# Half-precision products that nobody reads, placed in TensorE's waits: the last feed-forward part of each stack, and the norm with the latents

## What is computed

```python
x = x + 0.5 * ffn_ref(layernorm(x), ...)   # a stack of 6 layers
x = x + attn_ref(layernorm(x), ...)        # latent attention, 16 heads
x = x + 0.5 * ffn_ref(layernorm(x), ...)   # the same stack again

# one layer of the stack: 16 heads of 64, keys in windows of 32
x = attn_layer(shift_tokens(x), Wqkv, qs, ksc, Wo) + x
x = ffn_layer(shift_tokens(x), g, bln, W1, b1, W2, b2) + x

def ffn_layer(x, g, bln, W1, b1, W2, b2):
    mu = x.mean(-1, keepdims=True)
    var = ((x - mu) ** 2).mean(-1, keepdims=True)
    xn = (x - mu) / jnp.sqrt(var + 1e-05) * g + bln
    hg = xn @ W1 + b1                       # 128 -> 2 * 341
    a, gate = jnp.split(hg, 2, -1)
    return a * jax.nn.gelu(gate, approximate=False) @ W2 + b2

# latent attention begins with
kv_c = x @ W_kv                             # 128 -> 32
kv_c = kv_c * rsqrt(mean(kv_c * kv_c) + 1e-6) * g_kv
q_c = x @ W_q                               # 128 -> 64
```

## Time and profile before

| | |
|---|---|
| median of 3 runs | 5265.4 us (5253.43 to 5268.99) |
| the profiled execution, its own time | 5250.07 us |
| its span, first to last instruction | 5247.9 us |
| mean granted TensorE clock | 0.951 of full speed |
| TensorE busy | 4961.6 us (95%) |
| DVE, ACT, POOL busy | 73%, 68%, 69% |
| first tail, mean product to barrier | about 2001.5 to 2035.7 us of the span |
| norm with the latents | about 2038.4 to 2102.2 us |
| second tail | about 5204.5 to 5237.8 us |

### The profile page before, as it was taken

The page is one execution under the profiler, slowest core; times in us unless marked ns, Lnnn a source line. Parts: engine busy times, 40 slices in busy tenths (PEclk is TensorE's granted clock), DMA queues, the critical chain, the costliest instruction groups (busy, mean ns, idle before and its releaser), DMA issues. The chain is left out here.

```text
span 5247.9 us, 143424 instructions
## 1 busy us (share of the span) xinstructions
PE 4961.6 (95%) x46348; PEld 3103.1 (59%) x46348; DVE 3839.2 (73%) x8399; ACT 3594.2 (68%) x10738; POOL 3597.6 (69%) x4498
## 2 busy tenths in 40 slices
PE   7999999999999997899999997999999999999998
PEld 4666666666666663344444443666666666666665
DVE  5888878888788882455555555888878888788885
ACT  4888888888888882133333332888878878788785
POOL 6988888888888882211111123988888888888884
PEclk8999999999999996598988898999999999999998
DMA  2122122221212211000000001122121221212211
GB/s 74 47 58 52 45 60 50 56 54 47 58 49 60 50 47 20 5 3 3 3 3 3 3 3 48 48 51 59 45 60 48 53 56 44 60 48 56 53 45 34
DMA packets 296849, 217.73 MB, mean 41 GB/s; under 512 B 82028, under 2 KB 293608, under 8 KB 295144
## 3 DMA queue, kind: packets, MB, share of 16 engines
q1 hardware_dynamic: 296072, 208.01, 15.8%
HBM read 40.83 MB, written 1.05 MB: 8 GB/s over the span
## 5 line engine op out<-in xcount | busy, mean ns | idle before, releaser
L541 POOL TENSOR_TENSOR inv<-ssm,neg_half 128x8 f32<-128x8 f32 x768 | 1364.3, 1776 | 119.8 <-DVE ssm L860 55.3
L555 POOL TENSOR_TENSOR rot<-t 128x256 f32<-128x256 f32 x1536 | 1124.6, 752 | 335.8 <-DVE t L849 267.2
L732 ACT ACTIVATE prob<-ps,nmx,inv 128x96 f32<-128x96 f32 x3072 | 1288.1, 434 | 55.7 <-DVE nmx L846 44.0
L628 PE MATMUL ps<-w_qkv,xs 128*128 128x512 f32 x1536 | 874.3, 652 | 59.1 <-issue 28.8
L1361 ACT ACTIVATE ptl<-ps_l 128x1024 f32<-128x1024 f32 (+1 forms) x288 | 281.2, 977 | 707.9 <-PE ps_l L1222 560.3
L835 DVE TENSOR_REDUCE mx<-ps 128x4 f32<-128x384 f32 x768 | 424.5, 553 | 385.6 <-PE ps L655 382.9
L732 ACT ACTIVATION_READ_ACCUMULATOR prob<-ps,nmx,inv 128x1 f32 x3072 | 632.1, 206 | 0.0
L725 ACT COPY vt<-ps 128x256 f32<-128x256 f32 x768 | 286.4, 373 | 470.3 <-PE ps L666 458.7
L819 DVE TENSOR_TENSOR t<-ps,tab_s 128x256 f32<-128x256 f32 x1536 | 573.1, 412 | 36.2 <-issue 28.4
L827 DVE TENSOR_TENSOR prob<-prob,rec 128x384 f32<-128x384 f32 x768 | 562.6, 732 | 26.4
L716 ACT ACTIVATE sq<-ps 128x512 f32<-128x512 f32 x768 | 472.9, 616 | 109.1 <-PE ps L628 107.4
(11 more groups left out here) (192 smaller groups left out, 8291.2 us busy)
## 6 DMA issues: line engine op xcount, KB each, us to landing
vs<-vt SPq DMA_DIRECT2D x768, 96.0 KB, 2.2
vs<-vt SPq DMA_DIRECT2D x768, 64.0 KB, 2.0
vs<-vt SPq DMA_DIRECT2D x768, 32.0 KB, 1.8
xs<-x_a SPq DMA_DIRECT2D x384, 32.0 KB, 1.9
w_qkv<-in_L_ffn_Wqkv SPq DMA_DIRECT2D x48, 256.0 KB, 3.8
w_qkv<-in_L_ffn_Wqkv SPq DMA_DIRECT2D x48, 128.0 KB, 3.1
w_o<-in_L_ffn_Wo SPq DMA_DIRECT2D x12, 512.0 KB, 4.1
w<-in_L_ffn_W SPq DMA_DIRECT2D x12, 341.0 KB
```

The source lines that it names most:

```text
L541: nc.gpsimd.tensor_tensor(inv[:, n % 4], ssm[:, n % 2], neg_half[:, 0:2 * HU], ALU.pow).then_inc(z["inv_ready"], 1)
L555: nc.gpsimd.tensor_tensor(rot[:, n % 4, half[w]], t1[:, n % 2, half[w]], t2[:, n % 2, half[w]], ALU.add).then_inc(z["rotated_" + w], 1)
L628: pe.matmul(ps[:, j % 2, :], xs[:, j // UT % 2, :], w_qkv[:, 0:2, u * 256:(u + 1) * 256], start=True, stop=True).then_inc(z["qk_ready"], 1)
L732: e = nc.scalar.activation(prob[:, n % 2, h, :], scores[:, h % 2, h // 2, :], ACT.Exp, scale=inv[:, n % 4, h:h + 1], bias=nmx[:, n % 2, h: ...
```

## The change

Two local functions `spare` issue products of the half-precision identity with itself, repeated four times: 128 rows, 512 columns out, no semaphore, result never read. In the stacks they write bank 0, which only the queries' and keys' product uses, and they are issued only in the slots `j >= UNITS + LAG_Y`, that is in the tail. The three added waits are for the last readers of banks 0 and 1. In the norm with the latents they write bank 7, which is first used by the rotation.

```diff
@@ window_stack, block.tensor
             pe.wait_ge(z["consts_ready"], 8 + 2 * (k + 1))
+
+
+            def spare(count):
+                for n in range(count):
+                    pe.matmul(ps[:, 0, :], ident_h[:, :], ident_h[:, :].unsqueeze(1).to_broadcast([P, 4, P]), start=True, stop=True)
+
+            SPARE = {"mean": 4, "var": 6, "spread": 5, "gate": 2, "up": 2, "down": 8}
 
             def feed_forward(L, p, g):
...
                 if p is not None:
                     feed_forward(L, p, g)
+                    if j >= UNITS + LAG_Y:
+                        if p == PHASE["mean"]:
+                            pe.wait_ge(z["squared"], (L + L0 + 1) * UNITS)
+                            pe.wait_ge(z["t1_ready"], (L + L0 + 1) * UNITS)
+                            pe.wait_ge(z["t2_ready"], 2 * (L + L0 + 1) * UNITS)
+                        for name, count in SPARE.items():
+                            if p == PHASE[name] or (name in ("gate", "up") and p in PHASE[name]):
+                                spare(count)
                 if live(LAG_P):
@@ latent_attention, block.tensor
+            def spare(count):
+                for n in range(count):
+                    pe.matmul(ps[:, 7, :], ident_h[:, :], ident_h[:, :].unsqueeze(1).to_broadcast([P, 4, P]), start=True, stop=True)
+
+
             for n in range(G + 2):
                 if n < G:
                     norm_mean(nc, z, pe, nb, mean_w, q0 + n, n)
+                if n == 0:
+                    spare(4)
                 if 1 <= n <= G:
                     norm_var(nc, z, pe, nb, mean_w, q0 + n - 1, n - 1)
+                if n == 1:
+                    spare(6)
                 if n >= 2:
                     latents(n - 2)
                 if 1 <= n <= G:
                     norm_spread(nc, z, pe, nb, ones_w, q0 + n - 1, n - 1)
                 if n >= 2:
                     latent_squares(n - 2)
+                    spare(6)
                     latent_spread(n - 2)
+                    if n > G:
+                        spare(4)
```

## The result

The changed kernel takes 5224.67 us (median of 7 runs, 5217.76 to 5239.88), the kernel before beside it 5262.21 us (7 runs, 5245.57 to 5268.99). The ratio is 0.9938 with a 95% interval of 0.9918 to 0.9958: faster by 0.6%, some 33 us by the ratio and 37.5 by the two medians. The profiled execution took 5234.97 us (span 5232.8), 15.1 us less than that of before; it is one of the slower of the seven, and that of before one of the faster.

A forecast was written before the change was run, and what follows sets the result against it. TensorE bounds the kernel, 95% busy, with its clock halved in places. Tails 12.4, norm 8.5 and decoding 4.5 sum to 25.4 us off the profiled 5250.07; against the median of 5265.4 that gives 5240 us, range 5223 to 5262.

The forecast's parts named there:

- The tails: Both stacks' tails: full clock gives back 17.4 us, less 2.0 for spares and 3.0 for half-clock stretches, 12.4 us.
- The eight: Spares behind each tail's down product: they delay the barrier and the mix by about 1.0 us, 2.0 for both stacks.
- one short half-clock stretch per tail: In each tail the clock still falls once for a short stretch, costing 1.5 us each, 3 us for both.
- the weakest spot: First up product in the tail: its two spares end some 2 us before the gelu lets the second up go.
- The norm: Norm with the latents, from the first latents on: faster products at full clock save 8.5 us.
- The 60%: Norm with the latents: share taken of the remaining 14.1 us, because one wait of about 1.5 us has no spares.
- The decoding: Decoding behind the norm: full clock lasts about five us of the 22.84 us at half clock, saving 4.5 us.
- every fall follows a stretch in which TensorE mostly waited: Reading of the earlier trace's clock falls, used to argue that spares filling about 60% of each tail wait hold the clock.
- an edit ahead of it may shift that by some us either way: Attention: places where the clock rises and falls hang on small shifts; some us either way, nothing booked.
- The clock falls again and again: Rival, 15%: clock falls at gelu, mix and an unfilled norm wait, returning late; 12 us less gain, 5253 us.
- The full clock throughout, decoding included: Rival, 15%: full clock holds through tails, norm and decoding until the rotation's waits; 41 us less, 5224.5 us.
- The spares stand in the way: Rival, 10%: half-precision spares fail to hold the clock and outlast waits in tails and norm; 16 us more, 5281 us.

The follow-up runs named there:

- e1_tails: The change with spares in the two tails alone, none in the norm with the latents: 5239.8 us, ratio 0.9946 against the kernel before.
- e4_no_eight: The change without the eight spares behind the down product of each tail: 5222.73 us, ratio 0.9905 against the kernel before.
- c1_tiny: The change with every spare in its place but one column wide in place of 512: ratio 0.9976 against the kernel before.
- p1_ahead: The kernel before plus 35 one-column products in the first tail alone, ahead of the second stack's loop: ratio 0.9962 against the kernel before.
- c2_after: The change itself run again, unaltered: ratio 0.9916 against the kernel before, 43 us faster.
- e2_norm: The change with spares in the norm with the latents alone, none in the tails: 5238.95 us, ratio 0.9937 against the kernel before.
- e3_rows32: The change with every spare from 32 rows in place of 128, same number, place and length: 5261.7 us, ratio 0.9978 against the kernel before.

## Why the prediction was right, and where it was not

The direction, the chance given to it and the range held. The forecast of 5240 us lies 15 us above the measured time. Part of that is 3.6 us more in the booked stages; the larger part is a gain that no term named.

**The tails (12.4 us booked).** Measured 7.2 and 6.2 us in the profiles, 13.4 together, and 13.4 again with the tails alone (e1_tails). The eight were booked at 2.0 for both; e4_no_eight gives 1.8, by the drain that was named; the mix follows the down product's end by 2.0 us, as forecast. The one short half-clock stretch per tail was there too. In the profile of the change it lies ahead of the first spares, at the last output product and the mean; in its repetition, and in 9 of the 14 tails with these spares, it follows the gelu's wait, the weakest spot that was named. Its price in the tail is the same at either place: 0.95 on the mean (2.07 against 1.12), or 0.9 on the third up (2.00 against 1.09). The longer L645 (3.05 and 3.78 against 2.05) lies ahead of the tail, and in the first stack the kernel before had 3.51 there. Booked were 1.5 a tail, the price of L638: this term was too large by about half a microsecond a tail, which accounts for 13.4 in place of 12.4.

**The norm (8.5 booked, bounds 5 to 14).** Measured 10.7, 8.6 in the repetition and 8.8 alone. The DMA held the first latents as forecast (16.1 us is their distance from the norm's first mean, not, as the prediction has it, from the mix's end, which is 16.4). The 60% stood for falls at the unfilled wait behind the spread of the scale. That wait is 1.54 us at 2080.27 in the change, and no fall came there. In the repetition the clock is 0.50 for 3.42 us from 2083.34, right behind the same wait, so the wait named is a real risk, and there the stage came out at the 8.5 booked.

**The decoding (4.5 booked).** Measured 4.9 and 4.0. The clock fell 5.4 us after its start, where five were assumed from the short stretches of the earlier trace rows. That the two agree is in part luck: the repetition had 4.5 us.

**The sum of the booked terms** was 25.4 and came to 29.0. So the mechanism was right and the sizes within their bounds. One reading under it was not: that every fall follows a stretch in which TensorE mostly waited. In the earlier trace rows the clock falls at 2062.08 after 1.91 busy of 3.41 us, and again behind the stretch of 5.09 busy of 6.83; in the changed kernel it fell in the decoding with no gap at all.

**The step that failed** is "an edit ahead of it may shift that by some us either way", which looked for side effects in the attention only and booked nothing. Instructions that do no work, ahead of the second stack's loop, were worth 0.24% (c1_tiny) and 0.38% (p1_ahead) of the whole time, 13 and 20 us; in the profiles the loop's four returns are 7.6 us shorter with the change. The 29.0 us of the stages and these 7.6 come close to the 37.5 us between the two medians, but that is luck and no closed account: the same pair of profiles has 3.1 us more ahead of the first tail and 13.3 more in the attention. The firm comparison is c2_after against c1_tiny, 27.8 us, for which the stages give 24.9. The halves fit less well: e2_norm has 12.5 us of stages and 33 measured, with 26 at the end of its interval, against about 19 from stages and returns. Where the surplus arises stays open in part; the attention, which took 1062.7 to 1084.0 us over these profiles, hides it.

**The rivals.** *The clock falls again and again*: it falls, once in each tail and once in the norm of the repetition, but only for 3.4 to 6.8 us each time, and comes back. *The full clock throughout, decoding included*: its time (5224.5) is nearly the measured one, but by luck, since the surplus stands in it for what the decoding did not give. The tails did nearly as it said; the decoding, its largest term over the forecast, fell to half after 5.4 us without a gap. The rule of the Trainium skill behind it, "TensorE: Matmul & The Clock Gate", section "Why this matters for your kernels", ties a fall to long idle gaps between bursts. The traces disagree twice: the decoding fell with TensorE busy 17.79 of 17.79 us, and the tails of before were at half with no wait over 2.08 us. *The spares stand in the way*: refuted for 128 rows, and reproduced with 32 (e3_rows32). The prediction suspected half precision; what matters here is the rows.

## What to carry to other kernels

Where TensorE's clock is at half in a stretch of short serial products, products of full height that nobody reads, placed in its waits and a little shorter than them, bring the full clock back for most of it at next to no cost on the path; check that they run from all 128 rows, and put none ahead of a barrier. Where TensorE has no waits to fill they cost what they win, as in the attention. Price such an edit by the stretch that it touches, and then measure an inert twin of it (same instructions, one column) beside it: here the twin alone gave 0.24% where the change beside it gave 0.84%, and that part does not come from the clock that the spares hold. Two halves whose gains sum to more than the whole are the sign to look for that.

## What the runs showed of the hardware that was not expected

- A dense queue of products does not hold the clock by itself. Spares from 32 rows kept TensorE busy 34.30 of 34.73 us at a clock of 0.51; from 128 rows, busy 21.95 of 27.03, it was 0.93.
- At each return of a loop TensorE stands still (2.77 us in the attention, 3.67 and 3.91 in the second stack, with no releaser), and the clock then falls, in the stack for 3.4 or 6.8 us, twice for 10.2. In the second stack this goes with instructions elsewhere in the program: with none added ahead, 6.8 us or more at 12 of 12 returns; with inert ones ahead, 3.4 at 6 of 8.
- One and the same kernel loses the clock at different places from one execution to the next: in the tail ahead of the first spares (the change) or behind a wait of 2.03 us (c2_after), for the same 29.8 and 29.7 us.
- Products queued ahead of a return run on during it: 18 spares took 4.04 us, and the next product followed without idleness, though 1.0 us later than without them.
- The attention of one and the same kernel took 1067.9 and 1078.9 us in two profiles, so a difference of ten microseconds there, read from one pair of profiles, means nothing.
